# Router logits from extra columns of the value product, one root for three norms, idle products ahead of the experts, and another order of products and transposes

## The reference, cut to what matters

```
z = layernorm(patches) @ W_proj + b_proj          # 64 images x 36 patches of 768
h = concat(cls, layernorm(z)) + pos_emb           # 64 x 37 rows of 256
n = layernorm(h)
h = h + softmax(mask_diagonal(q k^T / 256)) v     # q, k, v from n, per image
m = layernorm(h)
logits = m @ router_w + router_b                  # 256 -> 8 experts
top 2 of 8, each expert keeps its 444 best rows   # capacity
h = h + layernorm(sum_e gate * (gelu(m @ w1[e] + b1[e]) @ w2[e] + b2[e]))
```

## Time and profile before

| | us |
|---|---|
| median of 3 runs | 420.9 (419.79 to 421.92) |
| the profiled execution | 419.44 |
| its span | 417.6 |
| busy PE / DVE / ACT / POOL | 347.9 / 316.1 / 258.7 / 243.1 |

### The profile page before, as it was taken

The page is one execution under the profiler, slowest core; times in us unless marked ns, Lnnn a source line. Parts: engine busy times, 40 slices in busy tenths (PEclk is TensorE's granted clock), DMA queues, the critical chain, the costliest instruction groups (busy, mean ns, idle before and its releaser), DMA issues.

```text
span 417.6 us, 8095 instructions
## 1 busy us (share of the span) xinstructions
PE 347.9 (83%) x2190; PEld 311.7 (75%) x2190; DVE 316.1 (76%) x868; ACT 258.7 (62%) x548; POOL 243.1 (58%) x435
## 2 busy tenths in 40 slices
PE   2789999999999999661024999999999999999940
PEld 0578889989899997450014899999999999999930
DVE  7676878788787865868889555778888888888772
ACT  3355777878777775445700378686868686868510
POOL 4167888878778876320005443258686868654574
PEclk9899999999999999955555699999999999999985
DMA  5632034454535398578713487557777777652221
GB/s 176 188 83 64 20 93 130 133 137 125 149 115 144 102 118 146 147 187 244 10 0 88 140 225 198 151 156 209 213 210 213 212 211 214 208 179 57 66 77 54
DMA packets 49278, 58.38 MB, mean 140 GB/s; under 512 B 12167, under 2 KB 38007, under 8 KB 49244
## 3 DMA queue, kind: packets, MB, share of 16 engines
q1 hardware_dynamic: 42602, 43.11, 40.2%
q0 software_dynamic: 5568, 14.09, 12.6%
q10 hardware_dynamic: 1074, 0.79, 0.6%
HBM read 36.74 MB, written 21.36 MB: 139 GB/s over the span
## 4 chain that ended last, share of the span: by engine, by line
PE 76%; DVE 9%; issue 3%; DMA 3%; SPq 3%; POOL 3%; ACT 2%; DVEq 0%; POOLq 0%; ACTq 0%
PE pz L944 19%; PE pall L961 18%; PE pall L829 10%; PE pall L779 5%; PE pall L786 4%; PE pz L759 3%; DVE wproj L1228 3%; PE pall L804 2%; PE pall L812 2%; SPq L442 2%; PE pall L795 2%; PE pall L839 2%; PE pall L972 2%; PE pall L831 1%; PE pall L930 1%
## 5 line engine op out<-in xcount | busy, mean ns | idle before, releaser
L961 PE MATMUL pall<-halves 128*128 128x444 f32 x384 | 88.6, 365 | 0.8 <-DVE halves L1334 0.8
L944 PE MATMUL pz<-halves 128*128 128x444 f32 x384 | 89.1, 368 | 0.0
L944 PEld LDWEIGHTS pz<-halves 128*128 128x128 f32 x384 | 73.6, 192 | 5.1
L961 PEld LDWEIGHTS pall<-halves 128*128 128x128 f32 x384 | 70.8, 188 | 5.9 <-DVE halves L1334 1.1
L1574 POOL DMA_INDIRECT held<-x_rows,gidx x32 | 35.6, 1114 | 64.2 <-DVE gidx L1276 41.2
L712 ACT ACTIVATE wproj<-pz,b1t 128x444 f32<-128x444 f32 x64 | 40.5, 632 | 45.3 <-PE pz L944 45.3
L1334 DVE TENSOR_TENSOR halves<-wproj,halves 128x444 fp32r<-128x444 f32 x64 | 39.8, 622 | 28.4 <-ACT halves L724 28.4
L829 PE MATMUL pall<-halves 128*112 128x256 f32 x396 | 52.9, 288 | 3.6 <-DVE halves L1055 3.6
L1482 POOL TENSOR_TENSOR rs<-rs,neghalf 112x1 f32<-112x1 f32 x88 | 50.2, 570 | 7.3
L829 PEld LDWEIGHTS pall<-halves 128*112 128x112 f32 x396 | 48.6, 179 | 4.1 <-DVE zbias L1074 2.4
L1599 POOL DMA_INDIRECT out<-rows,didx x28 | 37.2, 1327 | 22.1 <-DVE rows L1382 15.3
(11 more groups left out here) (266 smaller groups left out, 716.5 us busy)
## 6 DMA issues: line engine op xcount, KB each, us to landing
stage<-in_w SPq DMA_DIRECT2D x32, 512.0 KB, 5.8
stage<-in_x SPq DMA_DIRECT2D x64, 108.0 KB
x_rows<-x SPq DMA_DIRECT2D x22, 224.0 KB, 3.1
x_rows<-held SPq DMA_DIRECT2D x22, 224.0 KB, 4.1
sums<-rows SPq DMA_DIRECT2D x7, 448.0 KB, 3.5
out<-held SPq DMA_DIRECT2D x21, 111.0 KB
x_rows<-zero SPq DMA_DIRECT2D x1, 1474.9 KB
wproj<-in_w_proj ACTq DMA_DIRECT2D x1, 768.0 KB
```

The lines of the kernel that those rows point to most:

```text
L944: m = nc.tensor.matmul(bank(k % 2)[:, 0:CAP], w[:, c, k * 128:(k + 1) * 128], xs[:, e % 2, c, 0:CAP], start=(n == 0), stop=(n == 3 * EC - 1))
L961: m = nc.tensor.matmul(pall[:, 2 * (e % 2) + o, 0:CAP], w[:, k, o * 128:(o + 1) * 128], hs[:, k % 2, 0:CAP], start=(k == 0 and n == 0), st ...
```

## The change

The router's product for a tile no longer has its own transposes and products. Eight centred router columns are appended twice to the value weights: once multiplied through the value weights (columns 256 to 263 of `v`, so that the attention output has eight more columns) and once as they are (the last eight columns of `v`, which give the logits' share of the rows before attention). ScalarE scales the latter by the row's deviation into `H` (`h_rw`), the residual sum `g_h` then runs over 264 columns, and ScalarE scales the last eight to logits (`LG`) in step i-4. The x2 transposes, their copy and the router product go. The preparation of these columns is added to steps 0 and 1.

The three roots of a step, `z` of i, `h` of i-1 and `g` of i-4, become one add and one power over up to three columns, after all three variances are there. The output bias add moves ahead of the position add on GpSimd.

In TensorE's order the patch product of i stands ahead of the x1 transposes of i-2. On ScalarE the copy of those transposes stands behind the exponentials.

Ahead of the first gathered rows TensorE runs 24 products of the identity with itself, whose result nobody reads.

```diff
         wqk = wq
-        wv = sb("wv", [128, EC, ED + 1])
+        HW = ED + E
+        VW = HW + 1 + E
+        wv = sb("wv", [128, EC, VW])
+        rwc = wv[:, :, HW + 1:VW]
         bqk = sb("bqk", [128, 2 * EC])
         tb = sb("tb", [128, EC])
-        bvb = sb("bvb", [P, ED + 1])
+        bvb = sb("bvb", [P, VW])
         amask = sb("amask", [P, P])
         rw = sb("rw", [128, EC, E])
         rbb = sb("rbb", [P, E])
...
+                    act.wait_ge(c_vT, 1)
+                    nc.scalar.copy(wvs[:, :, :], bank(5)[:, 0:EC * ED].rearrange("p (c e) -> p c e", c=EC)).then_inc(c_ws, 1)
+                    nc.scalar.copy(bvrep[:, :, :], bank(7)[:, 0:EC * P].rearrange("p (c r) -> p c r", c=EC)).then_inc(c_ws, 1)
...
+                    nc.scalar.copy(wv[:, :, ED:HW], bank(4)[:, 3 * EC:3 * EC + EC * E].rearrange("p (c e) -> p c e", c=EC))\
+                        .then_inc(c_tv, 1)
+                    nc.scalar.copy(bvb[:, ED:HW], bank(4)[0:P, 3 * EC + EC * E:3 * EC + EC * E + E]).then_inc(c_tv, 1)
...
                 t = i - 4
                 if live(t):
-                    plain(act, (x2T_ps, t - 1), (x2_out[slot], 16 * (t // 4) if isinstance(t, int) else (t - slot) * 4),
+                    plain(act, (n_rs, i + 1), (g_h, t + 1))
+                    nc.scalar.activation(LG[:, :, at(t)] if not isinstance(t, int) else LG[:, :, t:t + 1],
+                                         tile_of(H, t, ED, HW).rearrange("p (e a) -> p e a", a=1), ACT.Copy,
+                                         scale=norm(par, 1, 2)).then_inc(l_sb, 1)
+                    plain(act, (x2_out[slot], 16 * (t // 4) if isinstance(t, int) else (t - slot) * 4),
                           (g_nb, t + 1))
-                    nc.scalar.activation(x2[:, slot, :], tile_of(H, t), ACT.Identity, bias=rs[:, 3, 2:3],
-                                         scale=rs[:, 3, 1:2]).then_inc(x2_ok, 1)
-                t = i - 1
-                if live(t):
-                    need(act, x1T_ps, t + 1)
-                    need(act, s_ps, t - 1)
-                    nc.scalar.copy(x1T[:, odd, :], bank(6)[:, 0:EC * P]).then_inc(x1T_sb, 1)
+                    nc.scalar.activation(x2[:, slot, :], tile_of(H, t), ACT.Identity, bias=norm(par, 2, 2),
+                                         scale=norm(par, 1, 2)).then_inc(x2_ok, 1)
...
+                t = i - 2
+                if live(t):
+                    plain(act, (h_dev, t + 1), (v_sb, t + 1))
+                    nc.scalar.activation(tile_of(H, t, ED, HW), v[:, par, HW + 1:VW], ACT.Copy, scale=dev[:, odd:odd + 1])\
+                        .then_inc(h_rw, 1)
+                t = i - 1
+                if live(t):
+                    need(act, x1T_ps, t + 1)
+                    need(act, s_ps, t - 1)
+                    nc.scalar.copy(x1T[:, odd, :], bank(6)[:, 0:EC * P]).then_inc(x1T_sb, 1)
...
-                        m = nc.tensor.matmul(bank(4)[0:P, 0:ED + 1], xt_[:, c, :], wv[:, c, :],
+                        m = nc.tensor.matmul(bank(4)[0:P, 0:VW], xt_[:, c, :], wv[:, c, :],
...
-                t = i - 6
-                if live(t):
-                    need(pe, x2T_sb, t + 1)
-                    need(pe, l_sb, t)
-                    need(pe, z_2, i if not isinstance(i, int) else min(i, TILES))
-                    for c in range(EC):
-                        m = nc.tensor.matmul(bank(2)[0:P, 256:256 + E], x2T[:, c * P:(c + 1) * P], rw[:, c, :],
-                                             start=(c == 0), stop=(c == EC - 1))
-                    m.then_inc(l_ps, 1)
...
+                t = i
+                if live(t):
+                    need(pe, xT_lo, t + 1)
+                    need(pe, z_2, t)
...
+                    nc.tensor.matmul(bank(2)[0:P, 0:ED], ones2[:, :], zbias[:, :], start=False, stop=True)\
+                        .then_inc(z_ps, 1)
...
-                t = i
-                if live(t):
-                    need(pe, xT_lo, t + 1)
-                    need(pe, z_2, t)
-                    need(pe, l_sb, t - 5)
...
-                t = i - 5
-                if live(t):
-                    need(pe, x2_ok, t + 1)
-                    need(pe, x2T_sb, t)
-                    need(pe, t_sb, t + 3 if not isinstance(t, int) else min(t + 3, TILES))
-                    for c in range(EC):
-                        m = nc.tensor.transpose(bank(3)[:, 256 + c * P:256 + (c + 1) * P],
-                                                x2[:, (slot + 3) % 4, c * 128:(c + 1) * 128], ident[0:P, 0:P])
-                    m.then_inc(x2T_ps, 1)
...
+                    for o in range(EC):
+                        for c in range(EC):
+                            nc.tensor.transpose(bank(5)[:, o * ED + c * 128:o * ED + (c + 1) * 128],
+                                                wv[:, c, o * 128:(o + 1) * 128], ident[:, :])
+                    for c in range(EC):
+                        nc.tensor.transpose(bank(7)[:, c * P:(c + 1) * P], bvb[:, c * 128:(c + 1) * 128], ident[0:P, 0:P])
+                    pe.wait_ge(c_idx, 2)
+                    for c in range(EC):
+                        m = nc.tensor.matmul(bank(6)[:, 0:E], onesf[:, :], rw[:, c, :], start=(c == 0), stop=(c == EC - 1))
+                    m.then_inc(c_vT, 1)
...
+                    pe.wait_ge(c_ws, 4)
+                    pe.wait_ge(c_rw, 1)
+                    for c in range(EC):
+                        for o in range(EC):
+                            nc.tensor.matmul(bank(4)[:, 3 * EC + c * E:3 * EC + (c + 1) * E],
+                                             wvs[:, o, c * 128:(c + 1) * 128], rwc[:, o, :],
+                                             start=(o == 0), stop=(o == EC - 1))
+                    for o in range(EC):
+                        m = nc.tensor.matmul(bank(4)[0:P, 3 * EC + EC * E:3 * EC + EC * E + E], bvrep[:, o, :], rwc[:, o, :],
+                                             start=(o == 0), stop=(o == EC - 1))
...
+            def keep_clock(n):
+
+                for _ in range(n):
+                    nc.tensor.matmul(bank(3)[:, 0:128], ident[:, :], ident[:, :], start=True, stop=True)
+
...
+            keep_clock(24)
             for h in range(2):
...
+                    V_.memset(bvb[:, HW + 1:VW], 0.0)
+                    dve.wait_ge(c_vT, 1)
+                    V_.scalar_tensor_tensor(rwc, rep(bank(6)[:, 0:E].rearrange("p (a e) -> p a e", a=1), 1, EC),
+                                            -1.0 / ED, rw[:, :, :], ALU.mult, ALU.add).then_inc(c_rw, 1)
...
+                    plain(dve, (r_inv, t + 1), (h_rw, t + 1))
+                    V_.scalar_tensor_tensor(tile_of(H, t, 0, HW), bank(7)[0:P, 0:HW], rinv[:, 0:1], tile_of(H, t, 0, HW),
                                             ALU.mult, ALU.add).then_inc(g_h, 1)
...
-                t = i - 1
-                if live(t):
-                    need(pool, x1_ok, t)
-                    scaled(2, hmv, h_mv, t + 1, h_rs0, h_rs, h_nb)
-                t = i
-                if live(t):
-                    need(pool, z_sc, t)
-                    rstd(1, zmv, z_mv, t + 1, z_rs0, z_rs)
-                t = i - 4
-                if live(t):
-                    need(pool, x2_ok, t)
-                    scaled(3, gmv, g_mv, t + 1, g_rs0, g_rs, g_nb)
...
+                par = slot % 2
+                on = [k for k, back in enumerate((0, 1, 4)) if live(i - back)]
+                if on:
+                    a, b = on[0], on[-1] + 1
+                    if 0 in on:
+                        need(pool, z_sc, i - 1)
+                    if 1 in on:
+                        need(pool, x1_ok, i - 2)
+                        need(pool, h_rw, i - 2)
+                    if 2 in on:
+                        need(pool, x2_ok, i - 5)
+                        need(pool, l_sb, i - 5)
+                    plain(pool, *[((z_mv, i + 1), (h_mv, i), (g_mv, i - 3))[k] for k in on])
+                    G.tensor_scalar(nrm[:, par, 0, a:b], nmv[:, a:b, 1], EPS, None, ALU.add).then_inc(n_rs0, 1)
+                    need(pool, n_rs0, i + 1)
+                    G.tensor_tensor(nrm[:, par, 1, a:b], nrm[:, par, 0, a:b], rep(neghalf[:, :], 1, b - a), ALU.pow)\
+                        .then_inc(n_rs, 1)
+                    plain(pool, (n_rs, i + 1))
+                    for k, done in ((1, h_nb), (2, g_nb)):
+                        if k == 1 and k in on:
+                            G.tensor_tensor(dev[:, par:par + 1], norm(par, 0, 1), norm(par, 1, 1), ALU.mult).then_inc(h_dev, 1)
+                        if k in on:
+                            G.tensor_scalar(norm(par, 2, k), nmv[:, k, 0:1], norm(par, 1, k), -1.0, ALU.mult, ALU.mult)\
+                                .then_inc(done, 1)
+                t = i - 5
+                if live(t):
+                    if isinstance(t, int) and t == 0:
+                        pool.wait_ge(c_l, N_L)
+                    need(pool, x2_ok, t + 1)
```

(28 more changed lines are left out.)

95 lines of the change are left out of this document (36 added, 59 removed).

## The result

The changed kernel takes 417.78 us (median of 4 runs, 417.16 to 418.13), the kernel before, measured beside it, 421.07 (419.79 to 421.92). The ratio is 0.993, 95% interval 0.9907 to 0.9953. Forecast were 409.5 and a range of 406.0 to 414.0: the sign is right, the size is less than a third of it. The profiled execution took 417.94 (span 416.1) against 419.44 (span 417.6), 1.5 less, where 11.4 less was forecast.

A forecast was written before the change was run, and what follows sets the result against it. TensorE was taken to bound the loop, always busy at full clock. Loop -7.7, early steps 0, last steps -1.5 and idle products -2.2 sum to -11.4 us, giving 409.5 us, range 406.0 to 414.0.

The forecast's parts named there:

- The cycle through the position add and `hstat` back to `zstat`: Loop step, across VectorE, GpSimd and ScalarE: this cycle was taken as shorter than the others, some 5.7 us.
- TensorE in a step: Loop: x2 transposes (0.34) and router product (0.31) go, wider products add 0.06; step 6.67 to 6.08, taken as 6.12 us.
- The batched root: GpSimd's joint root in a step: `x1` can start 3.3 us after the patch product; power of three columns 0.89.
- ScalarE to the x1T copy: ScalarE's row in a step, from `x1` through the x1T copy: 3.3 us, ending 6.6 after the patch product.
- The two-step chain: Loop: root, x1T copy, query-key product to patch product, `zstat`: 11.9 to 12.1 us, or 5.97 to 6.06 a step.
- Steps 0 to 6: Before the loop: step 1's added narrow instructions and later roots offset by savings; sum 0, bounds -1 and +1.5 us.
- Last steps: After the loop: last tiles' logits 2.7 us earlier, gates ahead of them free 1.5 earlier; -1.5, bounds 0 and -2.7.
- Idle products: Ahead of the experts: 24 products raise TensorE's clock, first output product comes earlier; -2.2 us, bounds +0.7 and -3.5.
- rival 2: TensorE's clock falls back ahead of the experts, or rises late: 412.4 us, chance 0.12.
- Rival 1: Loop: the root's chain binds in full, by larger lags or a slower power; step 6.3, 413.0 us, chance 0.18.
- Rival 3: Loop: x1T copy not ready, TensorE waits ahead of the query-key product; step 7.1, 423.3 us, slower, chance 0.03.
- Rival 4: Loop: another wait fills the 0.65 us freed on TensorE; loop gives 0 to -1, 416.5 us, chance 0.05.

The follow-up runs named there:

- experiment 14: The kernel before with all 28 steps written out instead of a loop of four: 422.32 us, ratio 1.0035.
- experiment 9: The changed kernel with all 28 steps written out on every engine instead of a loop of four: 412.37 us, ratio 0.979.
- 1: The changed kernel with the root of `h` by itself again, only the roots of `z` and `g` batched: 413.83 us, ratio 0.9819.
- 8: The changed kernel with the root of `h` by itself and GpSimd's constant tables moved ahead of step 0: 411.09 us, ratio 0.9765.
- experiment 6: The changed kernel with the patch product of i behind the x1 transposes of i-2 again: 425.01 us, ratio 1.0099.
- Experiments 3: The changed kernel with the 8 wide products of step 1 moved between the narrow ones: 419.56 us, ratio 0.9952.
- experiment 4: The changed kernel without the 24 idle products: 418.96 us, ratio 0.994.
- fillers: Five more idle products ahead of each of the last three pairs of gathered transposes, in two variants of the changed kernel: 414.66 and 412.34 us.
- 7: The kernel before with the 24 idle products alone added: 418.64 us, ratio 0.9948.

## Why the prediction was wrong

**The step that failed** is the one that set a second bound aside: "The cycle through the position add and `hstat` back to `zstat` is shorter, some 5.7." Written out it is 5.60 to 5.81, so the 5.7, given without its working, fits a kernel without a loop. In the loop it is 6.40, and 7.08 where it passes the loop's turns. Left out was what the loop adds to each of its eight links, 0.8 in all, what a turn adds, 0.68 once, and what `nmax`, held up by the position add, adds where VectorE would otherwise be waiting, 0.07 in the loop and 0.2 written out. On TensorE's own row the loop costs nothing (experiment 14: 6.67 and 6.68). It costs only in a ring of latencies that no queue covers, and the batched root closed such a ring at nearly TensorE's length. It was worth -2.7 instead of -7.7.

The waits of GpSimd and ScalarE, 60 us of the changed kernel, show it by name; written out `x1` has no wait on issue (`x` for `x1` is L610 there, 6.0 us in 9 waits for the root):

```profile
POOL nrm L1563 <- DVE nmv L1162: 9.8, 10, 1.4
ACT x L616 <- issue: 8.1, 7, 1.4
```

**TensorE in a step**: right. 6.08 and 6.12 were forecast; once the ring was shorter, 6.09 to 6.14 was measured in each step of 9 and 6.14 as the mean of 1 and of 8. `tT` without the router product's cover cost nothing.

**The batched root**: right in its parts, too early in its start. Power 0.88 (0.89 forecast), deviation 0.19 (0.2). Product's end to `x1`: 3.2 written out (102.36 to 105.53), 3.3 forecast; in the loop 3.9 (106.69 to 110.56), of which 0.4 is VectorE late for `zstat` (107.10), forecast at 0.2 at most.

**ScalarE to the x1T copy**: 3.3 forecast, 3.40 measured. The two-step chain through it was worked out with most care and did not bind: VectorE's row behind `v` had 0.4 to 0.7 to spare.

**The move of the patch product**: right, and needed: 7 us (experiment 6).

**Steps 0 to 6**: 0 forecast, bounds -1 and +1.5. +0.6 where the clock held (9), +2.5 in the changed kernel. Of the 1.9 between them, 1.5 is the half clock in step 2, which no part of the forecast had.

**Last steps**: -1.5 forecast; -1.5 in experiment 9, -2.0 in 1 and 8, -0.1 in the changed kernel. There, behind the last tiles, the clock fell again, windows of the changed kernel 6 and 9 us behind the patch product of step 21:

```profile
161.46:164.46 3.00, 1.73 (x10) 0.92 (x9) 2.29 (x11) 2.65 (x9) 1.48 (x3) 1.00 0.90 100
164.46:167.46 3.00, 3.00 (x14) 2.42 (x13) 0.44 (x1) 1.69 (x5) 2.32 (x6) 0.57 0.77 190
```

Experiments 3 and 4 show the same two windows, 9 shows the first at 1.74 busy and then 1.00 of the clock.

**Idle products**: -2.2 forecast; -1.3 in the changed kernel, -0.5 to -1.9 in the others without fillers where the clock held (-1.8 and -1.9 in 7 and 8), +0.9 to +2.7 where it fell back. The lower bound of -3.5 was added up wrongly: 1.6 and 2.3 less 0.7 are 3.2. Both the forecast and rival 2 happen, in different executions. For the Trainium skill's sentence on transposes (TensorE: Matmul & The Clock Gate, Part 4) the rows say: the clock outlived 8 transposes and two lists at 1.31 each in the changed kernel, so the gain is not lost by them alone.

**Rivals.** Rival 1 had the right name ("the root's chain binds in full"), the wrong ring (the copy of x1T) and too small a price: 6.3 where 6.48 came. Its 413.0 set the upper end of 414.0, which was 3.8 too low. Rival 3's step (6.93) came when the order was turned back (6.95), but not its mechanism: TensorE waited there for `x1` ahead of the transposes, not for their copy. Rival 4 fell.

## What to carry to other kernels

In a software pipeline with an engine that is always busy, list every ring of hand-overs that closes within one step, and price it by starts read in the same loop, link by link, never by durations. Here each link cost about 0.1 us more in a register-addressed loop than written out (0.8 over eight), and a turn 0.7 more once, which shows only when the ring is as long as the busy engine's work. Joining operations that become ready at different times (here three roots) saves engine time and lengthens the ring by the wait for the last: ask first which engine time is short.

## What the runs showed of the hardware

- GpSimd's power of three columns takes 0.88 us, in line with 0.57, 0.72 and 1.04 for one, two and four.
- VectorE's `nmax`, one column from two operands, takes 0.10 to 0.11 us in most of the steps of the kernel before. Between 20 and 180 us of the 18 profiles it took 0.2 us or more 147 times, up to 0.74, and each time it ended 0.00 to 0.03 us after a 256-column add on GpSimd that was under way. Where it started within 0.1 us of the position add's start it was not held. It did so in the loop and written out alike.
- TensorE's clock fell to half while TensorE was busy behind 32 products of 1 to 8 columns. With equal code in the prologue this came in some executions (the changed kernel) and not in others (experiment 4), and the patch product of step 2 took 3.6 to 4.2 us where it takes 2.35.
